# Expert layer of a two-layer transformer kernel: routing weights read back from DRAM by broadcast loads in place of selection products, down products one chunk later and in two banks

## What is computed

```python
logits = x @ gate_w.T                       # 8 experts
w = softmax(logits); keep the top 2, divide by their sum, 0 elsewhere
y  = sum over e of w[e] * ((silu(x @ wg[e]) * (x @ wu[e])) @ wd[e])     # inner width 176 each
y += (silu(x @ swg) * (x @ swu)) @ swd                                  # shared, inner width 352
```

## Time and profile before

| What | Value |
|---|---|
| runs | 1714.83, 1717.16, 1717.18 us; median 1717.16 us |
| span of the profiled execution (first to last instruction) | 1708.8 us; the page gives no other time for it |
| median less this span | 8.4 us |
| window attention of layer 0 | about 40 to 261 us of the span |
| expert stage, prologue (splitting the weights) | 261.9 to 276.3 us |
| expert stage, first gate matmul to last down matmul | 276.3 to 555.6 us |
| everything after it | from 557 us on |

### The profile page before, as it was taken

One profiled execution on the slowest core, in us unless ns is written; L12 is line 12 of the kernel. 1 busy time (PEld: TensorE's weight loads), 2 busy tenths in 40 slices (PEclk: granted clock), 3 DMA queues, 4 the chain that ended last, 5 costly groups with the idle time before them and its releaser, 6 DMA issues. The chain is left out here.

```text
span 1708.8 us, 44008 instructions
## 1 busy us (share of the span) xinstructions
PE 1513.5 (89%) x16988; PEld 1164.6 (68%) x16988; DVE 1319.0 (77%) x2187; ACT 1217.6 (71%) x2065; POOL 1099.4 (64%) x661
## 2 busy tenths in 40 slices
PE   5899996999999499999999578899999999999885
PEld 4677774677776266666666467777777777777774
DVE  5899974555655699999997788887888888888753
ACT  2677774545445488888888378888888888888873
POOL 1777752555555388888887477776676777667614
PEclk8899998999999699999999689999999999999997
DMA  5000000000000500000000001111111110111113
GB/s 174 2 3 3 3 3 15 15 8 7 7 7 1 185 2 2 14 2 14 2 14 11 13 22 31 27 26 27 27 27 27 27 26 22 26 27 27 27 27 105
DMA packets 56837, 44.12 MB, mean 26 GB/s; under 512 B 28152, under 2 KB 47900, under 8 KB 56388
## 3 DMA queue, kind: packets, MB, share of 16 engines
q1 hardware_dynamic: 56644, 41.45, 9.1%
HBM read 17.75 MB, written 4.23 MB: 13 GB/s over the span
## 5 line engine op out<-in xcount | busy, mean ns | idle before, releaser
L831 POOL TENSOR_TENSOR a_prob<-a_prob,a_top 128x1024 f32<-128x1024 f32 x128 | 239.8, 1895 | 48.2 <-DVE a_top L1023 48.2
L1237 POOL TENSOR_TENSOR e_hh<-e_h,e_hh 128x512 fp32r<-128x512 f32 x112 | 144.8, 1293 | 146.6 <-ACT e_hh L1221 145.2
L1506 POOL TENSOR_TENSOR i_qk<-i_qk,i_rt 128x1024 f32<-128x1024 f32 x64 | 152.0, 2375 | 38.1 <-DVE i_rt L1955 33.3
L1516 POOL TENSOR_TENSOR i_qk<-i_qk,i_rn 128x1024 f32<-128x1024 f32 x64 | 122.5, 1915 | 80.5 <-DVE i_rn L1934 80.5
L1019 DVE TENSOR_TENSOR a_prob<-ps,a_table 128x1024 f32<-128x1024 f32 x128 | 149.7, 1211 | 23.4 <-PE ps L899 21.3
L1811 ACT ACTIVATE i_prob<-i_prob,i_top 128x128 f32<-128x128 f32 x512 | 156.4, 391 | 15.7 <-DVE i_top L1943 13.8
L977 ACT ACTIVATE a_probT<-ps 128x1024 f32<-128x1024 f32 x128 | 131.3, 1026 | 44.5 <-PE ps L907 44.5
L1258 DVE TENSOR_TENSOR e_h<-ps,e_sg 128x512 f32<-128x512 f32 x112 | 77.3, 690 | 104.3 <-PE ps L1120 90.4
L907 PEld LDWEIGHTS ps<-ident,a_prob 128*128 128x128 f32 x1024 | 113.2, 141 | 64.2 <-ACT a_probT L977 50.3
L1503 POOL TENSOR_TENSOR i_qk<-i_raw,i_rot 128x1024 f32<-128x1024 f32 x59 | 140.3, 2378 | 24.1 <-issue 24.1
L1208 ACT ACTIVATE e_sg<-ps 128x512 f32<-128x512 f32 x112 | 67.0, 598 | 123.2 <-PE ps L1120 122.4
(11 more groups left out here) (305 smaller groups left out, 4369.3 us busy)
## 6 DMA issues: line engine op xcount, KB each, us to landing
i_V<-i_V SPq DMA_DIRECT2D x96, 130.0 KB, 2.3
a_table<-skew_scratch SPq DMA_DIRECT2D x2, 2048.0 KB, 12.4
X<-in_L_attn_x SPq DMA_DIRECT2D x4, 512.0 KB, 6.1
a_table<-in_c_l_table SPq DMA_DIRECT2D x1, 2048.0 KB, 8.3
e_xs<-Y SPq DMA_DIRECT2D x8, 256.0 KB, 2.3
i_ms<-Y SPq DMA_DIRECT2D x16, 128.0 KB, 2.4
i_ms<-Y SPq DMA_DIRECT2D x16, 112.0 KB, 2.4
out_dram<-X SPq DMA_DIRECT2D x7, 256.0 KB, 2.3
```

Of the source, the lines that this page charges most:

```text
L831: nc.gpsimd.tensor_tensor(s, s, top[:, slot].unsqueeze(2).broadcast_to([P, HG, KW]), ALU.subtract).then_inc(shifted, 1)
L1237: nc.gpsimd.tensor_tensor(hh[0:n, slot(b, parity), 1, :], h[0:n, slot(b, parity), :], hh[0:n, slot(b, parity), 0, :].bitcast(F32), ALU.sub ...
L1506: nc.gpsimd.tensor_tensor(s, s, rt[:], ALU.add).then_inc(rotated, 1)
L1516: nc.gpsimd.tensor_tensor(flat, flat, rn[:, T // TPB % 2, T % TPB].unsqueeze(2).broadcast_to([P, 2 * FH, FD]), ALU.mult).then_inc(qk_done, 1)
```

## The change

- `choose_experts` loses parts 3 to 5 and writes the weights in fp32 as `chosen`, ordered round, expert, quarter. It is called at steps 4 and 12 alone.
- In the prologue of `experts` PE transposes `chosen` (two transposes), ACT copies them to `rows`, SP writes `rows` to DRAM (`rows_dram`, one row of 512 tokens for each round and expert) and waits until they have landed.
- `share` (128 x 11 x 512 fp32) takes the place of the route bank. SP fills it by loads that read one row of DRAM and write it on all partitions of an expert's piece of a chunk: 18 pieces a round, 11 chunks x 128 partitions x 2 KB = 2.88 MB. Chunk `s` of `share` is reloaded for the next round as soon as DVE has used it. DVE waits for chunks 0 to 5 together (10 pieces) and for chunks 6 to 10 together (8 pieces).
- DVE multiplies `sg` by `share` in place (both in SBUF) when the silu is done, and then the up bank by `sg`. The product with the route bank is gone.
- Gone too are `sel16`, its load and copy, two memsets on POOL, the staging, turning and copying of `ws`.
- Down products come three chunks behind (`BEHIND`), `hh` has 7 slots, and two banks (7 and 5) take the output in turn. The output transposes (bank 4) and the update of X move from s = 3 to s = 5 (`OUT`), the silu of the output to s = 3.

```diff
@@ choose_experts
-        nc.vector.tensor_tensor(wdense[:], wdense[:], bc(st), ALU.mult)
+        four = lambda a: a.rearrange("p (r q) e -> p r q e", q=4)
+        nc.vector.tensor_tensor(chosen[:].rearrange("p r e q -> p r q e"), four(wdense[:]), four(bc(st)), ALU.mult)
         dve.drain()
-    else:
-        v = part - 3
-        kept = wparts[:, :, NE * v:NE * (v + 1)]
-        nc.vector.tensor_copy(rounded[:], wdense[:])
...
@@ window_attention
-                if step >= 4 and step % 8 == 4 and step // 8 < 5:
+                if step >= 4 and step % 8 == 4 and step // 8 < 2:
                     between(dve, 1 + step // 8)
@@ new
+def expert_pieces(s):
+    edges = sorted({s * P, (s + 1) * P} | {e * INTER for e in range(NE) if s * P < e * INTER < (s + 1) * P})
+    return [(lo - s * P, hi - s * P, lo // INTER) for lo, hi in zip(edges, edges[1:])]
@@ experts, SP
-                sp.dma_start(ws[:, :, 0:3 * NE], wparts[:, bass.ds(i * 4, 4), :]).then_inc(staged, 16)
-            sp.wait_ge(cleared, 2)
+            def shares(i, s):
+                for lo, hi, e in PIECES[s]:
+                    sp.dma_start(share[lo:hi, s, :], rows_dram[bass.ds(i, 1), e, :].broadcast_to([hi - lo, N])).then_inc(share_in[s // FIRST_HALF], 16)
             stage(0)
+            sp.wait_ge(rows_sb, 1)
+            for v in range(2):
+                half = ROUNDS // 2
+                sp.dma_start(rows_dram[half * v:half * (v + 1)].rearrange("r e (q t) -> (r e q) t", t=P), rows[:, v, :]).then_inc(rows_out, 16)
+            sp.wait_ge(rows_out, 32)
+            for s in range(NR):
+                shares(0, s)
             with sp.Fori(1, ROUNDS) as i:
                 sp.wait_ge(x_T, i)
-                sp.wait_ge(w_T, i)
                 stage(i)
+                for s in range(NR):
+                    sp.wait_ge(shared_out, (i - 1) * NR + s + 1)
+                    shares(i, s)
@@ experts, PE
-                        if s < NR:
-                            after(pe, h2, i * NR + max(s - 1, 0))
-                            nc.tensor.matmul(ps[:, 4 + s % 2, :], sel16[:, a:a + n], wT[:, parity, :], start=True, stop=True).then_inc(route_ps, 1)
-                    if s == 3 and exists(i - 1):
+                    if s == OUT and exists(i - 1):
                         pe.wait_ge(out_sb, i)
+                        after(pe, x_new, i - 1)
...
-                        b, of = (s - 2, parity) if s >= 2 else (NC + s - 2, 1 - parity)
+                        b, of = (s - BEHIND, parity) if s >= BEHIND else (NC + s - BEHIND, 1 - parity)
                         n = CH[b][1]
-                        pe.wait_ge(h_lo, i * NC + s - 1)
+                        pe.wait_ge(h_lo, i * NC + s - BEHIND + 1)
                         if b == 0:
-                            after(pe, out_sb, i)
-                        split_product(ps[:, 7, :], (wd_hi[0:n, b, :], wd_lo[0:n, b, :]),
+                            after(pe, out_sb, i - 1)
+                        split_product(ps[:, down_bank(of), :], (wd_hi[0:n, b, :], wd_lo[0:n, b, :]),
@@ experts, ACT
-                        if s >= 1 and b < NR:
-                            act.wait_ge(h2, i * NR + b + 1)
-                        else:
-                            act.wait_ge(h1, i * NC + s)
-                        after(act, down, i * NC + s - HBUF)
+                        act.wait_ge(h1, i * NC + s)
+                        after(act, down, i * NC + s - HHBUF)
@@ experts, DVE
                         dve.wait_ge(gate_sb, i * NC + s + 1)
+                        if s < NR:
+                            if s % FIRST_HALF == 0:
+                                dve.wait_ge(share_in[s // FIRST_HALF], (i + 1) * (16 * HALF_PIECES[s // FIRST_HALF]))
+                            nc.vector.tensor_tensor(gate, gate, share[:, s, :], ALU.mult).then_inc(shared_out, 1)
+                            dve.drain()
                         dve.wait_ge(up_ps, i * NC + s + 1)
-                        nc.vector.tensor_tensor(hs, ps[0:n, 2 + s % 2, :], sg[0:n, s % 2, :], ALU.mult).then_inc(h1, 1)
-                        if s < NR:
-                            dve.drain()
-                            dve.wait_ge(route_ps, i * NR + s + 1)
-                            nc.vector.tensor_tensor(hs, ps[0:n, 4 + s % 2, :], hs, ALU.mult).then_inc(h2, 1)
+                        nc.vector.tensor_tensor(h[0:n, slot(s, parity, HBUF), :], ps[0:n, 2 + s % 2, :], gate, ALU.mult).then_inc(h1, 1)
```

More of the change, by code:

```diff
@@ L236, in router_buffers, with choose_experts @@
     wide = {n: sb(n, [P, NT, NE]) for n in ("lg", "rest", "first", "second", "wdense")}
-    return {**wide, "desc": sb("desc", [P, NE]), "st": sb("st", [P, NT]), "rounded": sb("rounded", [P, NT, NE], BF16)}
-def choose_experts(nc, dve, part, route, wparts):
-    lg, rest, first, second, wdense, desc, st, rounded = (route[n] for n in (
-        "lg", "rest", "first", "second", "wdense", "desc", "st", "rounded"))
+    return {**wide, "desc": sb("desc", [P, NE]), "st": sb("st", [P, NT])}
+def choose_experts(nc, dve, part, route, chosen):
+    lg, rest, first, second, wdense, desc, st = (route[n] for n in ("lg", "rest", "first", "second", "wdense", "desc", "st"))
     bc = lambda a: a[:, :].unsqueeze(2).broadcast_to([P, NT, NE])
@@ L273, in choose_experts @@
         dve.drain()
-    elif part == 2:
+    else:
         nc.vector.tensor_tensor(wdense[:], lg[:], first[:], ALU.mult)
@@ L1054, in experts @@
     ROUNDS = NBATCH * SEQ // N
-    wgu, wd, sel, loaded = weights
-    HBUF = 4
+    wgu, wd, loaded = weights
+    HBUF, HHBUF = 4, 7
+    BEHIND = 3
+    OUT = BEHIND + 2
+    TURNED, GATED = 6, 4
+    PIECES = [expert_pieces(s) for s in range(NR)]
+    FIRST_HALF = 6
+    HALF_PIECES = [sum(map(len, PIECES[:FIRST_HALF])), sum(map(len, PIECES[FIRST_HALF:]))]
+    rows_dram = nc.dram_tensor("chosen_scratch", (ROUNDS, NE, N), F32, kind="Internal").ap()
     with ExitStack() as c:
@@ L1169, in part @@
                                       b == 0, b == NC - 1).then_inc(down, 1)
+            for v in range(2):
+                half = chosen[:, NT // 8 * v:NT // 8 * (v + 1)].rearrange("p r e q -> p (r e q)")
+                last = nc.tensor.transpose(ps[:, GATED, v * P:(v + 1) * P], half, ident[:, :])
+            last.then_inc(rows_T, 1)
             fetch(0)
             pe.wait_ge(x_lo, 1)
-            fetch_w(0)
             pe.wait_ge(w_hi, 2)
             pe.wait_ge(w_lo, 3)
-            pe.wait_ge(sel_sb, 1)
@@ L1180, in _ @@
         def _(act):
+            act.wait_ge(rows_T, 1)
+            nc.scalar.activation(rows[:].rearrange("p v t -> p (v t)"), ps[:, GATED, 0:2 * P], ACT.Copy).then_inc(rows_sb, 1)
             nc.scalar.preload_act_table(ACT.Silu)
-            act.wait_ge(loaded, 16 * 8)
+            act.wait_ge(loaded, 16 * 7)
             nc.scalar.activation(wgu_hi[:], wgu[:], ACT.Copy).then_inc(w_hi, 1)
```

98 lines of the change are left out of this document (36 added, 62 removed).

## The result

The changed kernel takes 1674.72 us, the median of four runs (1673.37 to 1676.0), beside 1715.99 for the kernel before in the same runs (1714.58 to 1717.18): ratio 0.9767, interval 0.975 to 0.9784. The forecast was 1679, the range 1674 to 1694.

A forecast was written before the change was run, and what follows sets the result against it. PE was taken to bound the kernel; savings of 20.2 + 3.1 + 0.7 + 14.2 less 0.4 for stalls, 37.7 us, took the span from 1708.8 to 1671.1, with 8.4 added about 1679 us, range 1674 to 1694.

The forecast's parts named there:

- The bound: Expert stage: PE sets the pace, busy 34.1 of 35 us at full clock (2.4 GHz).
- Step and transposes: PE in the expert stage: each matmul costs 0.230 us, each set of four transposes 0.44 us.
- Route and weights: PE in the expert stage: dropping 88 route matmuls saves 20.2 us, seven sets of weight transposes 3.1 us.
- The waits, 14.2 us: PE in front of down products: with these three chunks behind, all 14.2 us of today's waiting goes.
- The wait left at chunk 8: PE's up product of chunk 8 waits for DVE, late from s = 5: 0 to 0.1 us a round, 0.4 added.
- DVE against POOL at no cost: Routed chunks: DVE's `share` product and POOL's operation share SBUF reading, 1.98 of 2.07 us; no cost, ends 0 to 18.
- the clock of one chunk: Expert stage: schedule of engine operations from a chunk's first gate matmul, 2.07 us a chunk; DVE and POOL miss each other.
- the 1.8 to 2.0 us in hand: Expert stage: slack before PE needs DVE's result (1.8 us) and POOL's (2.0 us), above the longest wait of 0.65.
- the rival: Routed chunks: shared reading port sets the pace, 0.16 us per DVE-POOL handover, 8 to 18 us lost, 1687 to 1697; chance 0.17.
- the 0.09 us a chunk of the sum: Routed chunks: margin by which DVE's and POOL's times kept apart still fit, 1.98 of 2.07 us.
- Loads, attention, prologue at no cost: Around and in the expert stage: loads hidden, 0; attention gain 0 to 1, taken 0; prologue cost 0, up to 4 us.
- From the span to the time: Whole kernel: sum made on the 1708.8 us span, then 8.4 us added, the span's distance below the median.

The follow-up runs named there:

- c_after: The changed kernel itself, unchanged, run again as a yardstick on the same chip: median 1675.43 us of five runs, ratio 0.978 to the kernel before.
- After: The changed kernel with the whole change against the kernel before, in its first measurement: median 1674.72 us of four runs, ratio 0.9767.

## Why the prediction was right, point by point

- **The bound.** Right. PE was busy 34.1 of 35 us and every matmul taken away came back as time.
- **Step and transposes.** Slightly low. A round of 30.10 less two sets at 0.42 and the wait of 0.12 is 29.14 us for 126 matmuls: 0.2313, where twelve of them in the earlier trace rows gave 0.230. Over 990 matmuls that is 1.3 us, which is nearly all of what the length after came out longer (237.7 for 236.4). A set costs 2.51 - 2.09 = 0.42, forecast 0.44.
- **Route and weights.** Right: 23.4 measured between the kernel with only the distance changed and the changed one, forecast 23.3.
- **The waits, 14.2 us.** The mechanism is right, the term somewhat too large. With 0.2313 the balance of before gives 274.1 - 250.0 - 8.8 - 2.1 = 13.2, since this term is what is left over, and a step too small makes it too large. The kernel with only the distance changed lost 12.9 us, with 0.7 of it the down product that moves to the tail, so about 12.2 of waits went. Term by term the saving is then 20.4 + 2.9 + 0.7 + 13.2 - 0.8 = 36.4, and 36.3 were measured.
- **The wait left at chunk 8.** Right in place, and 0.12 a round where 0 to 0.1 was expected (0.8 us in all for 0.4). Its reason was incomplete: DVE is late from s = 5, as said, but POOL on the port adds the last 0.17 us, and without the statistics the port alone holds it as long.
- **DVE against POOL at no cost.** Right to 0.4 us. The two do meet, which the clock of one chunk did not show: the mean of the product is 773 ns, not 690. The delays stay under the 1.8 to 2.0 us in hand, and the shared chunks end them. The kernel with 2.58 us of work for the port shows that the rival was real and what decided between them. The rival gave each handover a cost of 0.16 us; measured, the second operation ends 0.13 to 0.16 sooner than its own length after the first, so the margin was wider than the 0.09 us a chunk of the sum.
- **Loads, attention, prologue at no cost.** All three right: 5 MB a round cost nothing from round 1 on; the three parts are worth 0.03 us, which is no more than two executions differ by; the first gate product came 16.8 us after the attention in place of 17.0.
- **From the span to the time.** The weak step. The prediction added 8.4 us as if that much time lay around the span; around it lie 1.7 to 1.9. It did no harm, because span and 8.4 together are the median of before: 1717.2 - 37.7 = 1679.5 is the same sum, from medians throughout. With 1.9 in place of 8.4 the forecast would have been 1671.1 + 1.9 = 1673.0, too low, since the profiled execution of before was faster than most.
- **The forecast 1679 against the measured 1674.7.** This part owes something to luck. The stage saved 1.4 us less than forecast, yet the time came out 4.3 below the forecast and only 0.7 above the lower end of the range; two of the four runs lie under that end. With a saving of 36.3 the median of before gives 1680.9.
- **What stays open.** The medians differ by 41.3 us, the stage by 36.3. The interval of the ratio is 37 to 43 us and just leaves the stage's figure out; beside c_after the same difference is 1 - 0.978, or 38 us with 33.5 to 42.1 as ends, which holds it. The four experiments with nearly the same length and the same stretch before it (half of POOL's work, statistics late, more loads, parts back) have 0.9785 to 0.9794, 35 to 37 us. In the profiled executions what comes before the first reciprocal takes 61.7 to 64.6 us with the old route products and 61.8 to 66.7 without, and what comes after the last output transposes 1152.1 to 1155.5 and 1151.5 to 1157.4; neither shows a gain. I take the 5 us for scatter of what lies outside the stage, which these runs make likely and don't prove.

## What to carry to other kernels

When a consumer waits at a fixed distance behind its producer and the bound engine gets faster, the distance has to grow with it, or part of the gain comes back as waits: here the two edits gave 16.6 and 12.9 us alone and 36.3 together. Operand traffic that the bound engine carries (a matmul that only spreads values) can go to idle transfer engines; the price is then on whoever has to read the result, so where that makes VectorE read SBUF twice beside GpSimd, count the time of both together against the pace of the bound engine, one chunk at a time. Make a sum against the time of the same execution as the span, or against medians throughout, never across the two, and compare small edits by the length of the stage that they touch.

## What the runs showed of the hardware

- The exclusion between VectorE reading SBUF twice and GpSimd works both ways and per instruction: 0.69 became 1.22, 1.69 and 2.20 us on DVE, 1.29 became 1.54 and 1.61 on POOL, always 0.13 to 0.16 us short of a full wait. An operation of DVE with PSUM as one input kept 0.69 beside POOL.
- Broadcast reads of one 2 KB row of DRAM onto many partitions ran at 247 GB/s with the transfer engines full, and a piece of 256 KB landed 3.2 us (median) after its issue in the changed kernel. A plain load of that size (`e_xs`) took 2.3 before and 3.4 beside them.
- Where part of the scatter of whole times comes from. In the stretch from 20 to 40 us the granted clock differs from execution to execution. After and c_after have there (columns as the earlier trace rows):

```profile
20.00:40.00 20.00, 17.25 (x79) 15.51 (x79) 5.74 (x16) 5.96 (x13) 6.44 (x9) 0.57 0.24 63
```

```profile
20.00:40.00 20.00, 15.60 (x98) 12.63 (x98) 7.12 (x18) 6.46 (x14) 7.25 (x9) 0.73 0.25 68
```

In the first DVE began to add the bias table of the attention at 42.18 us, in the second, by the same program, at 38.72. Over the 14 profiled executions clocks of 0.51 and 0.52 go with 44.3 to 44.5 us, 0.73 to 0.83 with 38.6 to 38.7. The granted clock of the first is nearer to the lower of the two levels (1.2 and 2.4 GHz) there; in the 20 us before, PE was busy 8.3 of 20 in the first and 8.2 in the second, at 1.00 in both. Another part of the scatter lies after the expert stage, where the rest takes 1151.5 to 1157.4 us.
